# First attention with its rounded parts and rests stacked in 96 rows: one score product for a set of heads in place of three

## What is computed

```python
Q = query @ Wq + bq          # 32 heads of 16 values
K = key @ Wk + bk            # 8 heads of 16 values, each shared by 4 query heads
V = value @ Wv + bv
scores = jnp.einsum('bhgqd,bhkd->bhgqk', Q, K) * scale
w = jax.nn.softmax(scores, axis=-1)
y = jnp.einsum('bhgqk,bhkd->bhgqd', w, V)
return y @ Wo + bo
```

## Time and profile before

| | |
|---|---|
| median of 3 runs | 1883.62 us (1879.52 to 1884.27) |
| the profiled execution | 1882.03 us, its span 1880.2 us |
| PE busy | 1703.9 us, 91% of the span |
| DVE, ACT, POOL busy | 1206.0, 814.6, 1007.0 us |
| first attention after its projections | from 82.7 us to 263.4 us |

### The profile page before, as it was taken

The page is one execution under the profiler, slowest core; times in us unless marked ns, Lnnn a source line. Parts: engine busy times, 40 slices in busy tenths (PEclk is TensorE's granted clock), DMA queues, the critical chain, the costliest instruction groups (busy, mean ns, idle before and its releaser), DMA issues. The chain is left out here.

```text
span 1880.2 us, 27513 instructions
## 1 busy us (share of the span) xinstructions
PE 1703.9 (91%) x8898; PEld 1418.3 (75%) x8898; DVE 1206.0 (64%) x2393; ACT 814.6 (43%) x2591; POOL 1007.0 (54%) x1031
## 2 busy tenths in 40 slices
PE   3899966589999999999999999999999999997796
PEld 2778856368788887888788878888888777886684
DVE  5366655546776777766777775557666555655685
ACT  2088740124444444443344444444445444454342
POOL 2034320046666767766667676665666665662352
PEclk9889988589999999999999999999999999999895
DMA  3000010122221222211121122222222322220100
GB/s 130 23 1 1 0 39 1 41 62 63 61 68 56 68 68 73 63 57 57 51 62 55 59 79 68 62 70 72 62 67 77 87 74 74 73 79 6 58 18 28
DMA packets 57233, 104.10 MB, mean 55 GB/s; under 512 B 8016, under 2 KB 8528, under 8 KB 56976
## 3 DMA queue, kind: packets, MB, share of 16 engines
q1 hardware_dynamic: 55440, 99.27, 18.0%
q10 hardware_dynamic: 1664, 3.21, 0.5%
HBM read 100.36 MB, written 2.10 MB: 54 GB/s over the span
## 5 line engine op out<-in xcount | busy, mean ns | idle before, releaser
L83 POOL TENSOR_TENSOR a_w_lo<-a_raw,a_w_hi 128x512 fp32r<-128x512 f32 x186 | 240.9, 1295 | 14.9
L68 PE MATMUL ps<-a_wo_hi,a_oT_lo 128*128 128x512 f32 x544 | 227.2, 418 | 6.4 <-DVE a_oT_lo L83 4.9
L883 POOL CAST a_w_hi<-a_raw 128x512 fp32r<-128x512 f32 x186 | 115.3, 620 | 208.5 <-PE ps L70 208.4
L70 PE MATMUL ps<-a_wo_hi,a_oT_hi 128*128 128x512 f32 x544 | 215.3, 396 | 0.0
L69 PE MATMUL ps<-a_wo_lo,a_oT_hi 128*128 128x512 f32 x544 | 213.9, 393 | 0.0
L890 POOL TENSOR_TENSOR a_probs<-a_probs,a_total 128x512 f32<-128x512 f32 x128 | 135.9, 1061 | 142.3 <-DVE a_total L1314 141.9
L1151 ACT ACTIVATE a_v_hi<-ps 128x128 fp32r<-128x128 f32 x128 | 35.5, 278 | 365.4 <-PE ps L999 365.4
L83 POOL TENSOR_TENSOR a_wo_lo<-a_raw,a_wo_hi 128x512 fp32r<-128x512 f32 x128 | 165.7, 1295 | 10.3
L1289 DVE TENSOR_TENSOR a_cross<-ps,a_cross 128x512 f32<-128x512 f32 x128 | 88.1, 689 | 127.4 <-ACT a_cross L1137 124.9
L83 DVE TENSOR_TENSOR a_pT_lo<-ps,a_pT_hi 128x512 fp32r<-128x512 f32 x192 | 128.7, 684 | 40.6 <-ACT a_pT_hi L2092 21.3
L1298 DVE SCALAR_TENSOR_TENSOR a_probs<-a_cross,a_q_scale,a_mask 128x128 f32<-128x128 f32 x256 | 148.1, 637 | 0.0
(11 more groups left out here) (408 smaller groups left out, 5041.7 us busy)
## 6 DMA issues: line engine op xcount, KB each, us to landing
a_raw<-in_L_wq SPq DMA_DIRECT2D x128, 256.0 KB, 2.6
a_raw<-in_L_wo SPq DMA_DIRECT2D x128, 256.0 KB, 2.6
a_raw<-in_L_wkv SPq DMA_DIRECT2D x64, 256.0 KB, 2.6
a_raw<-in_L_main SPq DMA_DIRECT2D x12, 256.0 KB, 3.0
setup_raw<-in_cT SPq DMA_DIRECT2D x4, 512.0 KB, 7.2
x<-in_x ACTq DMA_DIRECT2D x8, 256.0 KB, 9.0
t_c_raw<-in_context SPq DMA_DIRECT2D x8, 256.0 KB, 5.8
out<-x SPq DMA_DIRECT2D x8, 256.0 KB, 2.0
```

The costliest lines, as they stand in the source:

```text
L68: pe.matmul(out, lhs_lo, rhs_hi, start=start, stop=False)
L70: return pe.matmul(out, lhs_hi, rhs_hi, start=False, stop=stop)
L83: return eng.tensor_tensor(out_lo, value, hi.bitcast(F32), ALU.subtract)
L883: pool.tensor_copy(hi, r).then_inc(s["chunk_hi"], 1)
```

## The change

Two new pairs of tiles of 96 rows, `q_stack` and `k_stack`. For each item SP issues 24 transfers from SBUF to SBUF (function `stack`): for each of the 4 rounds and each of the three combinations hi-hi, lo-hi and hi-lo of queries and keys, the 32 rows of the queries (512 columns, 64 KB) and the 32 rows of the keys (256 columns, 32 KB) are copied into rows 0 to 31, 32 to 63 and 64 to 95. SP waits before them for `q_lo` and `k_lo` of the item, and for the scores of the item two before. The sum over 96 rows is then the sum of the three products, and `scores` issues one product for a set, 4 in a round, where it issued 12. PE waits at a new item for `stacked`, all 24 transfers of it, where it waited for `q_lo` and `k_lo`. `stage_qk` on ACT waits for the transfers of the item two before, where it waited for its scores.

```diff
--- before.py
+++ after.py
@@ -1855,6 +1855,7 @@
 KV0 = 8
 SETS = 4
 ROUNDS = KV0 // 2
+PAIR = 2 * HD0
 RH = 2 * SETS
 RW = RH * S
 
@@ -1953,12 +1954,15 @@
         probs = [ph.sb(f"probs{p}", RW) for p in (0, 1)]
         pT = [ph.split(f"pT{p}", RW) for p in (0, 1)]
         raw_max, neg_max, total = ([ph.sb(f"{n}{p}", RH) for p in (0, 1)] for n in ("raw_max", "neg_max", "total"))
+        q_stack = [ph.sb(f"q_stack{p}", ROUNDS * SETS * S, F32R, 3 * PAIR) for p in (0, 1)]
+        k_stack = [ph.sb(f"k_stack{p}", ROUNDS * 2 * S, F32R, 3 * PAIR) for p in (0, 1)]
         oT, keep = ph.split("oT", SETS * S), ph.sb("keep", 2)
-        s = ph.sems("wo_in wo_hi wo_lo keep zeroed q_hi q_lo k_hi k_lo v_hi v_lo s_mm raw_max neg_max exped inverse probs"
+        s = ph.sems("wo_in wo_hi wo_lo keep zeroed q_hi q_lo k_hi k_lo stacked v_hi v_lo s_mm raw_max neg_max exped inverse probs"
                     " pT_mm pT_hi pT_lo av_mm oT_hi oT_lo o_mm added")
         bank_s = [C.ps[:, 2 * BANK * p:2 * BANK * (p + 1)] for p in (0, 1)]
         bank_pT, bank_oT, bank_out = C.ps[:, 4 * BANK:6 * BANK], C.ps[:, 6 * BANK:7 * BANK], C.ps[:, 7 * BANK:8 * BANK]
         SCALE = HD0 ** -0.5
+        STACKED = 16 * 6 * ROUNDS
         block = ctx.enter_context(nc.Block())
 
         def items(eng, step):
@@ -1984,6 +1988,20 @@
         def _(sp):
             sp.dma_start(wo_raw[:, :], wo).then_inc(s["wo_in"], 16)
 
+            def stack(i, p):
+
+                sp.wait_ge(s["q_lo"], i + 1)
+                sp.wait_ge(s["k_lo"], 2 * (i + 1))
+                wait_from_one(sp, s["s_mm"], ROUNDS * (i - 1))
+                for r in range(ROUNDS):
+                    rows = slice(PAIR * r, PAIR * r + PAIR)
+                    for n, (q, k) in enumerate(((0, 0), (1, 0), (0, 1))):
+                        to = slice(PAIR * n, PAIR * n + PAIR)
+                        sp.dma_start(q_stack[p][to, blk(r, SETS * S)].bitcast(F32), q_s[p][q][rows, :].bitcast(F32)).then_inc(s["stacked"], 16)
+                        sp.dma_start(k_stack[p][to, blk(r, 2 * S)].bitcast(F32), k_s[p][k][rows, :].bitcast(F32)).then_inc(s["stacked"], 16)
+            for i in range(B):
+                stack(i, i % 2)
+
         @block.gpsimd
         def _(pool):
             def normalise(R, p):
@@ -2002,14 +2020,11 @@
             def scores(i, r, p):
                 R = i * ROUNDS + r
                 if r == 0:
-                    pe.wait_ge(s["q_lo"], i + 1)
-                    pe.wait_ge(s["k_lo"], 2 * (i + 1))
+                    pe.wait_ge(s["stacked"], STACKED * (i + 1))
                 wait_from_one(pe, s["exped"], RH * (R - 1))
-                rows = slice(32 * r, 32 * r + 32)
                 for n in range(SETS):
-                    last = matmul_split(pe, bank_s[r % 2][:, n * 2 * S:(n + 1) * 2 * S],
-                                        tuple(x[rows, n * S:(n + 1) * S] for x in q_s[p]),
-                                        tuple(x[rows, :] for x in k_s[p]), True, True)
+                    last = pe.matmul(bank_s[r % 2][:, n * 2 * S:(n + 1) * 2 * S], q_stack[p][:, blk(r * SETS + n, S)],
+                                     k_stack[p][:, blk(r, 2 * S)], start=True, stop=True)
                 last.then_inc(s["s_mm"], 1)
 
             def turn(i, r):
@@ -2065,7 +2080,7 @@
         def _(act):
             def stage_qk(i, p):
 
-                wait_from_one(act, s["s_mm"], ROUNDS * (i - 1))
+                wait_from_one(act, s["stacked"], STACKED * (i - 1))
                 act.activation(q_s[p][0][:, :], q32[:, bass.ds((i % B) * (SETS * S), SETS * S)], ACT.Copy).then_inc(s["q_hi"], 1)
                 for c in (0, 1):
                     act.activation(k_s[p][0][:, c * S:(c + 1) * S], k32[:, bass.ds((i % B) * S, S)], ACT.Copy,
```

## The result

| | before | changed |
|---|---|---|
| median | 1881.57 us (4 runs) | 1947.99 us (4 runs, 1945.52 to 1951.89) |
| ratio | | 1.0357, 95% interval 1.0327 to 1.0387 |
| profiled execution, span | 1882.03, 1880.2 us | 1945.52, 1944.0 us |
| the stage ends at | 263.4 us | 331.2 us |
| an item (key rest to key rest, mean of five) | 20.2 us | 28.3 us |

The kernel became 3.6% slower, by 66 us. The forecast was 1925 with a range up to 1948; with the ratio on the 1883.6 shown ahead of it the changed kernel stands at 1951, just outside (the median itself, 1947.99, lies on the upper bound). Sign, place and mechanism were right, one price was too low. In the two profiled executions the stage ends 67.8 us later and the span is 63.8 us longer: the part behind the stage, which is the same program, took 4.0 us less in the second, so single executions can't be compared closer than that.

A forecast was written before the change was run, and what follows sets the result against it. PE was taken to bound the attention stage, with ACT 3.1 us an item behind. With transfer waits, 95.5 + 8C + 6X + T = 306.3 against 263.4 us gave +42.9, thus 1925 us, range 1892 to 1948.

The forecast's parts named there:

- the price of an issue: Time on SP from one transfer's issue to the next: taken as 0.475 us, bounded by 0.38 and 0.53.
- C: Time from an item's key rest to the last landing of its 24 transfers: 23 x 0.475 + 2.3 = 13.2 us.
- The sum: End of the first attention stage: 95.5 + 8C + 6X + T = 306.3 us, against 263.4 before.
- X: Time from an item's first scores to the next key rest: 11.9 us, or 9.9 at full clock.
- T: Tail from the last item's first scores to the end of the stage: 33.8 us, against 32.8 before.
- one round at half clock: After each pause PE was taken to run one round at 1.2 GHz, adding 2.0 us to X.
- "About 6 us" of idle PE: PE was to stand idle about 6 us before each item's first scores, waiting for transfers, 8 times.
- Rival 1: PE's clock stays up in the attention stage: X = 9.9, T = 31.8, time 1911 us; chance 0.2.
- Rival 2: Transfers are hidden, C = 5.2 us, and ACT's 17.15 us bound an item: faster, 1862 us; chance 0.07.
- The estimate of 4.7 us for C: By the skill page's formula, C would be 2.0 + 2.7 = 4.7 us and the transfers would be hidden.
- Rival 4: SP's queue is slower still, with late landings: C = 18, X = 13.3, +91 us, 1973 us; chance 0.08.
- The price of the removed products: Eight fewer score products a round: PE loses 3.9 us an item, of which ACT allows at most 3.1.

The follow-up runs named there:

- run of forms: The change, but from item 2 on SP issues 24 transfers of another form for each item (HBM or SBUF source, 16 to 128 rows); 1935.97 us, a single run.
- early splitting: The change with queries and keys split three rounds earlier, still one wait for all 24 transfers; 1869.4 us, ratio 0.9960 against the kernel before.
- the way through HBM: The change with stacks made by four stores to HBM and six loads, 10 issues in place of 24; 1893.9 us, ratio 1.0081 against the kernel before.
- the products alone: The change with transfers for items 0 and 1 only, later items using those stacks; 1894.3 us, ratio 1.0099 against the kernel before.
- round waits: The change with each round waiting for its own 6 transfers and item 0 scored by the three products; 1870.5 us, ratio 0.9954 against the kernel before.

## Why the prediction was wrong, point by point

- **The step that failed is the price of an issue**: "tiny columns and 256 KB cost the same. None has 32 rows or SBUF as its source, so this price is bounded: 0.38 below, 0.53 above". It measured 0.633. The rows of before had one end in HBM without exception, and I made them the bounds of a form that they don't contain. Size, rows and columns indeed don't enter (shown by the run of forms), but SBUF at both ends does. C became 23 x 0.633 + 2.0 = 16.6 and not 13.2. With this C alone put into the sum the end is 333.5 and the time 1952, outside the range. 0.53 was not even the upper bound for HBM: the trace of before has one step of 0.79, which I had not looked at and whose cause is open (0.69 to 0.91 at the same place in the other runs):

```profile
265.57 0.74 SPq L320 DMA_DIRECT2D f_row<-in_L_ffn_ln_gamma  x1
266.36 0.49 SPq L320 DMA_DIRECT2D f_row<-in_L_ffn_ln_beta  x1
```

- **The sum was right for the rest.** With what was measured, it reads 94.1 + 8 x 16.6 + 6 x 11.8 + 33.3 = 331.0 against 331.2 (94.1, since this execution came to the stage 1.4 us earlier). Of the 24.9 us by which the stage ended later than forecast, 8 x 3.4 = 27.2 are C, less those 1.4 and about 1 that X and T were shorter.
- **X**, forecast 11.9, was 11.2 to 12.2, 11.8 in the mean; **T**, forecast 33.8, 33.3. The choice of one round at half clock was right: the clock fell in every pause and was back after 3 to 6 us. Rival 1 (the clock stays up) is refuted by the windows of the changed kernel.
- **"About 6 us" of idle PE**: 22.2 us before the first item (5.7 of them are there in the kernel before too), 10.2 before the second, 6.2 to 7.9 before the others. 8 waits, as said; 128 products, as said.
- **Rival 2** (transfers hidden, 1862): not in the change, but the early splitting shows its item, 17.15 us, exactly ACT's busy time. What hides them is not a faster queue but an earlier start, which I did not look for. In working out its condition I used two lengths for the stretch that the transfers have, 5.9 us and 7.3; with 5.9 the distance of two issues would have to be 0.16 and not 0.22. The estimate of 4.7 us for C beside it, from "DMA: Bandwidth & Descriptors" of the Trainium skill, is refuted too: C is 16.4 to 16.9. Of its two parts the fixed one, about 2.0 us, is what a landing takes here. That initiating a transfer is small beside it does not hold here, 0.63 us 24 times. The section gives its formula for transfers that GpSimd issues, and these are issued by SP.
- **Rival 4** (the queue is slower still) said C = 18, which is nearer to 16.6 than my 13.2, but for another reason: it made the landing late, and the landing was 2.0 us. Late landings came only on the way through HBM (4.5 in the median).
- **The price of the removed products** was taken by PE's busy time and ACT's, 3 us an item. It stood only for a kernel in which PE doesn't pause by the piece. In the change's own order of ACT it is 0.7 us. That did not hurt the forecast, since X was worked out from the chain and not from busy time, but it hurt two later expectations, by 15 us (the products alone) and by 5 (round waits).

What stays open: what exactly lets the clock fall in the rounds around `stage_qk`. The rows show no pause over 1.2 us there, and the kernel before has the same fall with no pause over 0.6 us from 118 to 219 us (0.50 from 182.9 to 186.1). Early splitting removes the pause in front of the scores and the dips together, and no run removed one without the other; the pauses in front of mixing, up to 1.1 us, stay in it and the clock stays up. Nor was a run made that issues the transfers from a second queue, and why SBUF at both ends makes an issue dearer no run shows.

## What to carry to other kernels

A transfer has three prices, the issue on its queue, the landing and the bytes; many small ones behind one wait cost the issues times their number, however idle the DMA engines are. Let each consumer wait for its own part, or start the chain one period earlier: either took over 70 us off here and made a loss a small gain, and both together with the old products for the first item made it 0.9%. Fewer issues help only until another price is the limit: with 10 issues through HBM it was the DMA engines. Take the price of an operation only from rows with the same kinds of operands at both ends; if there is none, the bound is open on that side.

## What was not expected of the hardware

- From one issue on SP to the next it is 0.63 us with SBUF as source and destination (0.55 the first step), with 16 to 128 rows and with 64 to 512 columns; with HBM at one end, as source or as destination, it is 0.47 (0.38 the first), but for single steps such as the one of up to 0.91 named above.
- Six loads from HBM of 256 and 128 KB into 32 rows each, right behind stores to the same place, landed after 4.5 us in the median with the DMA engines busy all the time at 215 to 221 GB/s; the stores, with 128 rows and pieces of the same size, had 362. The main stream's loads of 256 KB land after 2.6 us.
- PE's clock fell to half (0.91 over an item) with pauses of no more than 1.2 us between short products, transposes and mixing, and in four of five items that is worth 1.6 us of 19.8. In the kernel before it fell once from 118 to 219 us with pauses of no more than 0.6 us.
- Products with 96 rows follow one another at the same distance as with 32, 0.12 us at full clock (the kernel before from 147.85 us, the run with early splitting from 153.19) and 0.21 at half: four and the change to mixing take 0.48 us (153.19 to 153.67).
